# A four-layer attention and feed-forward kernel: a woven instruction order for the second and third layer, and narrow probability-times-value products in the fourth attention

## The reference

```
x = x + attn0(LN(x), ctx)   # 16 heads of 96, 4 key heads, keys = ctx and x
x = x + ffn0(LN(x))         # ternary weights, inner size 1376, cut to int8
x = x + attn1(LN(x), ctx)   # softmax(x ctx^T) ctx, no weights
x = x + ffn1(LN(x))         # z = x A^T; top 16 of 64 experts gate z; B z
x = x + attn2(LN(x), ctx)   # Q = x Wq^T + bq, K = ctx Wk^T + bk, values = ctx
x = x + ffn2(LN(x))         # three experts, two of them used, with gates
x = x + attn3(LN(x), ctx)   # RMS norm, 32 heads of 16 over 8 key heads, 64 keys
x = x + ffn3(LN(x))         # NF4 quantised and dequantised weights, inner 1376
```

## Time and profile before

| what | value |
|---|---|
| median of the runs | 1604.14 us |
| the profiled execution itself | 1597.06 us |
| its span, first to last instruction | 1595.2 us |
| mean granted TensorE clock | 0.935 of full |
| PE busy | 1379.0 us, 86% |
| DVE busy | 1016.7 us, 64% |
| ACT busy / POOL busy | 461.2 us / 294.1 us |
| 16 DMA engines | 60 GB/s over the span |

### The profile page before, as it was taken

One profiled execution on the slowest core, in us unless ns is written; L12 is line 12 of the kernel. 1 busy time (PEld: TensorE's weight loads), 2 busy tenths in 40 slices (PEclk: granted clock), 3 DMA queues, 4 the chain that ended last, 5 costly groups with the idle time before them and its releaser, 6 DMA issues.

```text
span 1595.2 us, 18304 instructions
## 1 busy us (share of the span) xinstructions
PE 1379.0 (86%) x6285; PEld 1062.4 (67%) x6285; DVE 1016.7 (64%) x2281; ACT 461.2 (29%) x993; POOL 294.1 (18%) x170
## 2 busy tenths in 40 slices
PE   6559999999899998989966778689997777898998
PEld 5437776777677767867755457567886455677876
DVE  4567777767877775654587766773467499744241
ACT  3224334333333532422333102223213332321010
POOL 4101111111111211211112002215423311022120
PEclk9779999999999999999985899789998899899999
DMA  5521223313222331232112102200111100011001
GB/s 187 180 82 47 79 57 105 81 56 95 75 56 66 89 94 50 58 79 71 45 34 69 58 22 60 71 19 27 53 53 54 39 0 1 1 53 53 24 19 53
DMA packets 99405, 96.37 MB, mean 60 GB/s; under 512 B 13138, under 2 KB 72418, under 8 KB 99314
## 3 DMA queue, kind: packets, MB, share of 16 engines
q1 hardware_dynamic: 98802, 94.35, 20.2%
q0 software_dynamic: 512, 0.85, 0.2%
HBM read 84.34 MB, written 10.82 MB: 60 GB/s over the span
## 4 chain that ended last, share of the span: by engine, by line
PE 63%; DVE 23%; issue 5%; DMA 3%; ACT 3%; SPq 3%; POOL 1%; ACTq 0%; DVEq 0%
PE bank L1688 47%; PE bank L2050 5%; PE bank L1782 4%; DVE nf_y L1630 4%; SPq L772 2%; DVE xn L1193 2%; PE bank L1715 1%; PE bank L1772 1%; DVE mx L1545 1%; PE bank L2013 1%; POOL slots L818 1%; DVE st L1266 1%; DVE st L1175 1%; DMA nf_a<-in_L_w 1%; DVE e L1548 1%
## 5 line engine op out<-in xcount | busy, mean ns | idle before, releaser
L1688 PE MATMUL bank<-xT,slots 128*128 128x512 f32 (+1 forms) x1920 | 459.7, 397 | 4.0 <-DVE xT L1152 2.1
L818 POOL TENSOR_TENSOR slots<-staging,slots 128x1024 fp32r<-128x1024 f32 (+4 forms) x97 | 228.4, 2357 | 1035.9 <-ACT slots L911 1035.9
L1688 PEld LDWEIGHTS bank<-xT,slots 128*128 128x128 f32 (+1 forms) x1920 | 349.5, 183 | 100.0 <-issue 7.6
L1630 DVE TENSOR_SCALAR nf_y<-nf_w 128x512 fp32r<-128x512 f32 (+2 forms) x495 | 252.3, 537 | 29.2 <-PE bank L2050 28.1
L1688 PE MATMUL bank<-slots,h 128*128 128x512 f32 (+1 forms) x728 | 179.9, 407 | 15.9 <-DVE h L1292 9.7
L2050 PE MATMUL bank<-nf_y,nf_d 128*128 128x512 f32 (+2 forms) x495 | 164.3, 415 | 13.7 <-DVE nf_y L1630 10.7
L1688 PEld LDWEIGHTS bank<-slots,h 128*128 128x128 f32 (+1 forms) x728 | 141.5, 195 | 52.0 <-DVE h L1292 10.5
L911 ACT ACTIVATE slots<-staging 128x1024 fp32r<-128x1024 f32 (+4 forms) x97 | 98.2, 1019 | 189.0 <-PE bank L1688 174.7
L945 ACT ACTIVATE e<-bank,mx 128x320 f32<-128x320 f32 x128 | 66.4, 523 | 235.4 <-DVE mx L1230 235.0
L2050 PEld LDWEIGHTS bank<-nf_y,nf_d 128*128 128x128 f32 (+1 forms) x495 | 92.6, 191 | 51.5 <-issue 19.1
L1782 PE MATMUL bank<-eT,v 128*96 128x256 f32 (+1 forms) x384 | 110.0, 408 | 0.3
(11 more groups left out here) (247 smaller groups left out, 1716.9 us busy)
## 6 DMA issues: line engine op xcount, KB each, us to landing
staging<-in_L_wqkT SPq DMA_DIRECT2D x16, 480.0 KB, 3.8
nf_out<-nf_w SPq DMA_DIRECT2D x30, 256.0 KB, 2.1
staging<-nf_out SPq DMA_DIRECT2D x30, 256.0 KB, 2.9
staging<-in_L_woT SPq DMA_DIRECT2D x16, 384.0 KB, 3.7
staging<-in_L_w SPq DMA_DIRECT2D x12, 512.0 KB, 3.9
nf_a<-nf_max SPq DMA_DIRECT2D x40, 128.0 KB, 3.5
nf_r<-nf_rcp SPq DMA_DIRECT2D x40, 128.0 KB, 3.4
nf_w<-in_L_w SPq DMA_DIRECT2D x15, 256.0 KB, 4.2
```

The lines of the kernel that those rows point to most:

```text
L818: g.tensor_tensor(lo, split_source(i), hi.bitcast(FP32), ALU.subtract).then_inc(*sig.mark("weight_low", i))
L1630: v.tensor_scalar(nf_y[0:rows, i % STAIR_RING, 0:size], w_, bound, first, compare, ALU.mult)\
L1688: ins = mm(dst, l_, r_, start=i == 0, stop=i == len(passes) - 1)
```

## The change

1. `schedule()` is rewritten for layers 1 and 2. `k2`, `c2`, `m2`, `c2t`, `z1(0)`, `route1(0)` and `gates1(0)` now stand inside attention 1. `turn(4,0)`, `raw1(2,0)`, `raw1(2,1)` and their `scores1` stand inside the last tiles of `z1/zt1/b1`. The chunks of `k2` and `m2` are loaded ahead of the others. In attention 2 both `stats` chains come early, and the first four `hid2` are those of half 0.
2. Waits and buffers: `h2` is four tiles instead of one; the wait of gate2 and of ACT's first `hid2` for the last NF4 store is now a wait of DVE at `hid2(0,0,1)`; `b1c` is loaded early; some tiles change their place.
3. Attention 3: seven of the eight `q3` products are spread, six of them over the first five units and one ahead of them. `scale3` is gone. `turn3` transposes the unscaled exponentials. `pv3` now makes, for each token tile and head pair, one product with `eT3` as stationary side and 34 columns of `vd3` moving: 32 value columns and 2 columns of ones, which give the sums. DVE takes the reciprocal of those sums and scales the result (`af3`), and the new step `back3` transposes it with 2 transposes a unit; ACT and DVE split that as `pv3` did.

```diff
 
-    steps += [("raw1", 1, 0), ("raw1", 1, 1), ("scores1", 1, 0), ("scores1", 1, 1), ("turn", 2, 1), ("probs1", 1, 0),
-              ("raw1", 1, 2), ("pv1", 1, 0), ("probs1", 1, 1), ("scores1", 1, 2), ("pv1", 1, 1), ("stats", 3, 0),
-              ("raw1", 1, 3), ("probs1", 1, 2), ("scores1", 1, 3), ("pv1", 1, 2), ("turn", 3, 0), ("probs1", 1, 3),
-              ("raw_route1", 0), ("pv1", 1, 3), ("stats", 3, 1)]
+    steps += [("k2", 0), ("raw1", 1, 0), ("raw1", 1, 1), ("k2", 1), ("scores1", 1, 0), ("bias2",), ("k2", 2),
+              ("scores1", 1, 1), ("turn", 2, 1), ("probs1", 1, 0), ("k2", 3), ("raw1", 1, 2), ("pv1", 1, 0),
+              ("probs1", 1, 1), ("raw1", 1, 3), ("c2",), ("scores1", 1, 2), ("pv1", 1, 1), ("stats", 3, 0),
+              ("m2", 0), ("probs1", 1, 2), ("scores1", 1, 3), ("m2", 1), ("pv1", 1, 2), ("m2", 2), ("turn", 3, 0),
+              ("raw_route1", 0), ("probs1", 1, 3), ("z1", 0), ("c2t",), ("route1", 0), ("pv1", 1, 3), ("m2", 3),
+              ("gates1", 0), ("stats", 3, 1)]
     if only == 3:
         return steps
 
-    steps += [("route1", 0), ("turn", 3, 1), ("raw_route1", 1), ("z1", 0), ("gates1", 0)]
+    after = {0: [("turn", 3, 1), ("raw_route1", 1)], 1: [("route1", 1)], 2: [("gates1", 1)],
+             4: [("stats", 4, 0)], 6: [("turn", 4, 0), ("raw1", 2, 0), ("raw1", 2, 1)],
+             7: [("scores1", 2, 0), ("scores1", 2, 1)]}
     for t in range(TILES):
-        if t + 1 < TILES:
-            steps.append(("z1", t + 1))
-        steps.append(("zt1", t))
-        if t >= 1:
-            steps.append(("b1", t - 1))
-        if t < 2:
-            steps.append(("route1", 1) if t == 0 else ("gates1", 1))
-        if t - 1 == TPH - 1:
-            steps.append(("stats", 4, 0))
-    steps += [("b1", TILES - 1)] + [("k2", c) for c in range(KT)] + [("bias2",), ("c2",), ("turn", 4, 0), ("stats", 4, 1)]
+        steps += [("z1", t + 1)] * (t not in (0, 6, 7)) + [("zt1", t)] + [("b1", t - 1)] * (t > 0) + after.get(t, [])
+        steps += [("z1", t + 1)] * (t in (0, 6))
+    steps += [("probs1", 2, 0), ("b1", TILES - 1), ("stats", 4, 1)]
     if only == 4:
         return steps
 
-    steps += [("m2", c) for c in range(KT)] + [("c2t",)]
-    steps += [("raw1", 2, 0), ("raw1", 2, 1), ("scores1", 2, 0), ("scores1", 2, 1), ("turn", 4, 1), ("probs1", 2, 0),
-              ("raw1", 2, 2), ("pv1", 2, 0), ("probs1", 2, 1), ("scores1", 2, 2), ("pv1", 2, 1), ("stats", 5, 0),
-              ("raw1", 2, 3), ("probs1", 2, 2), ("scores1", 2, 3), ("pv1", 2, 2), ("turn", 5, 0), ("probs1", 2, 3),
-              ("raw_gate2", 0), ("pv1", 2, 3), ("stats", 5, 1)]
+    steps += [("pv1", 2, 0), ("probs1", 2, 1), ("pv1", 2, 1), ("stats", 5, 0), ("turn", 4, 1), ("raw1", 2, 2), ("raw1", 2, 3),
+              ("scores1", 2, 2), ("scores1", 2, 3), ("turn", 5, 0), ("raw_gate2", 0), ("probs1", 2, 2), ("gate2", 0),
+              ("pv1", 2, 2), ("probs1", 2, 3), ("hid2", 0, 0, 0), ("pv1", 2, 3), ("stats", 5, 1)]
...
-    steps += [("gate2", 0), ("hid2", 0, 0, 0), ("turn", 5, 1), ("hid2", 0, 0, 1), ("raw_gate2", 1), ("gate2", 1)]
-    for i in range(2 * (KT - 1)):
-        steps += [("moe", i)] * (i < 4) + [("hid2", 0, 1 + i // 2, i % 2)]
+    steps += [("hid2", 0, c, 0) for c in range(1, KT)] + [("turn", 5, 1), ("raw_gate2", 1), ("hid2", 0, 0, 1), ("gate2", 1)]
+    steps += [("moe", 0), ("hid2", 0, 1, 1), ("moe", 1), ("hid2", 0, 2, 1), ("moe", 2), ("hid2", 0, 3, 1), ("moe", 3)]
...
-    steps += [("q3", 0, 0), ("turn", 6, 1)] + [("q3", c, 0) for c in range(1, KT)] + [("q3", c, 1) for c in range(KT)]
+    steps += [("q3", 0, 0), ("turn", 6, 1), ("q3", 1, 0)]
+    queries = {0: [("q3", 2, 0), ("q3", 3, 0)], **{c + 1: [("q3", c, 1)] for c in range(KT)}}
     units = [(b, c) for b in range(B) for c in range(KT)]
     steps.append(("keys3", 0, *units[0]))
     for n in range(len(units) + TURN3_LAG + 1):
         if n < len(units):
             steps.append(("scores3", n, *units[n]))
-        if 1 <= n <= len(units):
-            steps.append(("scale3", n - 1))
+            steps += queries.get(n, [])
+        if n > TURN3_LAG + 1:
+            steps.append(("back3", n - TURN3_LAG - 2, *units[n - TURN3_LAG - 2]))
         if n > TURN3_LAG:
             steps.append(("pv3", n - TURN3_LAG - 1, *units[n - TURN3_LAG - 1]))
         if 1 <= n <= len(units):
             steps.append(("values3", n - 1, *units[n - 1]))
         if TURN3_LAG <= n < len(units) + TURN3_LAG:
             steps.append(("turn3", n - TURN3_LAG, *units[n - TURN3_LAG]))
+        if n > TURN3_LAG + 1:
+            steps.append(("low3", n - TURN3_LAG - 2, *units[n - TURN3_LAG - 2]))
         if n > TURN3_LAG:
             b, c = units[n - TURN3_LAG - 1]
-            if b >= 1 and c < TPB:
-                steps.append(("o3", TPB * (b - 1) + c))
-            if (b, c) == (BPH, TPB - 1):
+            if b >= 1 and 1 <= c <= TPB:
+                steps.append(("o3", TPB * (b - 1) + c - 1))
+            if (b, c) == (BPH, TPB):
                 steps.append(("stats", 7, 0))
             if (b, c) == (BPH, KT - 1):
                 steps.append(("turn", 7, 0))
         if n + 1 < len(units):
             steps.append(("keys3", n + 1, *units[n + 1]))
+    steps += [(step, len(units) - 1, *units[-1]) for step in ("back3", "low3")]
...
+            chunk(("k2", i), P, (2, D), [((slice(None),), by_k(a["L2_wkT"], 2 * i, 2 * i + 2))])
...
-        for name, ap in (("z1", a["L1_aT"]), ("b1", a["L1_bT"]), ("k2", a["L2_wkT"]), ("m2", a["L2_wq"])):
+        for name, ap in (("m2", a["L2_wq"]), ("z1", a["L1_aT"]), ("b1", a["L1_bT"])):
...
-        h2 = sb("h2", [P, 2, 2, KT, TOK], F32R, l)
-        hf2 = sb("hf2", [P, 2, HALF], FP32, l)
+        h2 = {}
+        for block in ((0, 1), (1, 0), (1, 1)):
+            h2[block] = sb("h2_{}_{}".format(*block), [P, 2, KT, HALF], F32R, l)
...
+        sb("between", [P, 2330], FP32, l)
+        h2[0, 0] = sb("h2_0_0", [P, 2, KT, HALF], F32R, l)
+        hf2 = sb("hf2", [P, 2, HALF], FP32, l)
...
-        vd3 = sb("vd3", [P, 2, PAIRS, P], FP32, l)
+        vd3 = sb("vd3", [P, 2, PAIRS, PAIR3], FP32, l)
...
+        rc3 = sb("rc3", [P, TPB * PAIRS, 2], FP32, l)
+        af3 = sb("af3", [P, 2, TPB, P], FP32, l)
...
+                                     ("b1c", b1c[:], a["L2_b1"]),
...
+                    pool.wait_ge(*sig.when("vd3_clear", 0))
+                    for j in range(2):
+                        g.memset(vd3[CTX * j:CTX * (j + 1), :, :, 2 * HD3 + j], 1.0).then_inc(*sig.mark("vd3_ones", j))
+                        pool.wait_ge(*sig.when("vd3_ones", j))
...
-                i = (e * KT + c) * 2 + hf
-                if i == 0:
-                    for q in range(2):
-                        act.wait_ge(*sig.when(f"nf4_stored{q}", 3 * FT - 2 + (3 * FT - q) % 2))
+                i = 2 * KT * e + (hf * KT + c if e == 0 else 2 * c + hf)
                 act.wait_ge(*sig.when("hid2_product", (e, c, hf)))
                 act.wait_ge(*sig.when("loaded_b1c", 0))
                 if i >= 2:
                     e_, r_ = divmod(i - 2, 2 * KT)
-                    act.wait_ge(*sig.when("h2_low", (e_, r_ // 2, r_ % 2)))
+                    act.wait_ge(*sig.when("h2_low", (e_, r_ % KT, r_ // KT) if e_ == 0 else (e_, r_ // 2, r_ % 2)))
...
+                if (e, c, hf) == (0, 0, 1):
+                    for q in range(2):
+                        dve.wait_ge(*sig.when(f"nf4_stored{q}", 3 * FT - 2 + (3 * FT - q) % 2))
...
-            def scale3(n):
-                for i in range(TPB):
-                    dve.wait_ge(*sig.when("exp3", (n, i)))
-                    e = e3[:, n % E3_RING, i].rearrange("p (h k) -> p h k", h=HPC)
-                    hs = slice(i * HPC, (i + 1) * HPC)
-                    link(v.tensor_reduce(sm[:, n % 4, hs], e, AX.X, ALU.add))
-                    link(v.reciprocal(mx[:, n % 4, hs], sm[:, n % 4, hs]))
-                    v.tensor_tensor(e, e, mx[:, n % 4, hs].unsqueeze(2).broadcast_to((P, HPC, CTX)), ALU.mult)\
-                        .then_inc(*sig.mark("probs3", (n, i)))
-
             def pv3(n, b, c):
-                low("pv3", n, a3[:, b % 2, 1, c], psum(("pv3", n))[:, 0:S], a3[:, b % 2, 0, c])
+
+                dve.wait_ge(*sig.when("pv3_product", n))
+                pairs = psum(("pv3", n))[:, 0:TPB * PAIRS * PAIR3].rearrange("p (q m) -> p q m", m=PAIR3)
+                link(v.reciprocal(rc3[:], pairs[:, :, 2 * HD3:]))
+                if n >= 2:
+                    dve.wait_ge(*sig.when("back3_product", n - 2))
+                v.tensor_tensor(af3[:, n % 2].rearrange("p i (q h d) -> p (i q) h d", q=PAIRS, h=2),
+                                pairs[:, :, 0:2 * HD3].rearrange("p q (h d) -> p q h d", h=2),
+                                rc3[:].unsqueeze(3).broadcast_to((P, TPB * PAIRS, 2, HD3)), ALU.mult)\
+                    .then_inc(*sig.mark("scaled3", n))
+
+            def low3(n, b, c):
```

(19 more changed lines are left out.)

53 lines of the change are left out of this document (25 added, 28 removed), and 2 rows, old and new, of the table LAYER_STAGES.

## The result

| | before | changed |
|---|---|---|
| time, median of five runs each | 1605.4 us (1601.9 to 1609.4) | 1592.7 us (1588.8 to 1594.7) |
| ratio of the runs | 1 | 0.9923, 95% interval 0.9901 to 0.9946 |
| profiled execution, span | 1595.2 us | 1587.0 us |
| busy PE / DVE / ACT / POOL | 1379 / 1017 / 461 / 294 us | 1377 / 973 / 461 / 294 us |
| mean granted clock | 0.935 | 0.933 |

What follows compares the result with a forecast made beforehand. It took layers 1 and 2 to be bound by chains hopping between PE, ACT and DVE, and attention 3 by DVE, then PE. 1597.1 minus 24.5 minus 24 is 1548.6, scaled to 1555 us; range 1532 to 1582.

Steps and rivals of the forecast that it cites:

- unit of attention 3: Attention 3's loop: PE needs 4.5 us a unit, DVE about 4.2; the old unit was about 6.6 us.
- attention 3, stretch: From 1232.2 to the last `o3`: 116.6 us of PE plus 19 of waits, 136 us against 160.5 before.
- attention 3, whole: Attention 3 gains 24.5 us; bounds 9 to 32.
- k2, m2, c2 out of the open stretch: Behind the last `b1`: their 13 us of PE move into attention 1's idle time; PE pays nothing, DVE 3 us.
- `raw1(2,..)` into the loop, attention 2 rewoven: The turn, two `raw1` and scores cost the `zt1`/`b1` loop 5 us of PE; attention 2 becomes about 1 us worse.
- the NF4 jobs shift by a few: Background NF4 jobs move slightly along the schedule; counted as nothing.
- woven order in sum: Layers 1 and 2: 33 - 5 - 3 - 1 = 24 us gained; bounds 0 and 35.
- the narrow product gains PE nothing: Attention 3: stationary loads make the narrow product's passes take 1.8 us a unit, against 1.73 for the old values product.
- The first stall on the keys: Start of attention 3: `keys3(0)` stands behind a POOL split, so PE waits 5.3 us, plus 1.5 for half clock.
- attention 3's list of waits: Attention 3: first keys 5.3 and 1.5 us, `stats(7,0)` 4.5 and 1.7, end of loop 6; 19 us in all.
- 33 us leave the place: Behind the last `b1`: 28 us of k2, c2, turn, m2 and a DVE wait, plus 5.0 of `raw1`, leave the open stretch.
- My bound of 0: Layers 1 and 2 gain nothing, every filled gap returning as a DVE wait; rival "Only attention 3 pays", 15%, 1580 us.

Runs made afterwards that it cites:

- e5: e1 with each unit's masked keys handed out earlier, ahead of the weight splits on POOL: ratio to before 0.9860, 10.1 us better than e1.
- e1: The kernel before with the edits of attention 3 alone: ratio to before 0.9923, 12.3 us faster.
- e12: e9 with the old order again behind the last `b1` and in attention 2, k2, m2, c2 still in attention 1: ratio to before 0.9756, 1561.2 us.
- e9: The changed kernel with both repairs, NF4 jobs as in e3 and keys as in e5: ratio to before 0.9810, 18.1 us better than the changed kernel.
- e4: The kernel before with its sum of room fixed at 609.4, the changed kernel's value, which shifts its NF4 jobs: ratio to before 1.0088, 14.1 us slower.
- e3: The changed kernel with the sum of room fixed at 611.4, the old value: ratio to before 0.9885, 6.1 us better than the changed kernel.
- e2: The changed kernel with attention 3 as before: ratio to before 1.0021, 3.4 us slower.
- e18: e12 with each product of k2 and m2 made twice on PE, and through a shared helper those of `k3`: ratio to before 0.9763, 1.1 us over e12.
- e13: The kernel before with each product of k2 and m2 made twice at the old place, `k3`'s too: ratio to before 1.0024, 3.8 us slower.
- e11: e9 with one round instead of three in the statistics' reciprocal square root, `stats(2,0)` to `stats(5,1)`: ratio to before 0.9727, 13.3 us faster than e9.
- e7: e3 with the passage from attention 1 to the gated product ordered as before, k2, m2, c2 staying in attention 1: ratio to before 0.9891, no different from e3.

## Why the prediction was wrong, step by step

| step of the forecast | forecast | measured |
|---|---|---|
| unit of attention 3 | 4.5 us | 4.55 us |
| attention 3, stretch | 136 us | 146.8; 135.3 with keys ahead (e5) |
| attention 3, whole | -24.5 | -12.3 (e1); -22.4 (e5) |
| k2, m2, c2 out of the open stretch | part of -24 | -16.7 (e12 against e5, with the new order of `hid2` in it) |
| `raw1(2,..)` into the loop, attention 2 rewoven | -5 of PE to pay, about 1 worse | +8.7 (e9 against e12) |
| "the NF4 jobs shift by a few" | 0 | +14.1 (e4), 6.1 back in e3 |
| woven order in sum | -24 | +3.4 (e2); -8.0 with the NF4 jobs at their old places (e9 against e5) |

**Right.** DVE's sums leave, the bound of attention 3 passes to PE, and the narrow product gains PE nothing: 1.71 us against my 1.8. The issue-gap rule of the Trainium skill (TensorE: Matmul & The Clock Gate, Back-to-back issue gap) would have had 0.4 us there, and the measured 0.107 us per pass with its own stationary load decides for the rows. The first stall on the keys was 5.10 us, forecast 5.3. The end of the loop was 1.9 us of wait and 1.4 of clock, where I had 6. And PE indeed paid nothing in attention 1 for k2 and m2 (92.5 us with them doubled, e18, 92.9 without, e12).

**The first step that failed** is in one half-sentence: that the NF4 jobs' shift counts nothing. It was put at nothing without a reason, and cost 14.1 us by e4 and 6.1 by e3. The jobs are strung along the steps by a running sum of room. The new order ended that sum 2.0 lower, and jobs moved by a place or so all along the list, hundreds of us ahead of the edit. One of them has a DMA wait of 9 us on DVE (already in the trace of before), harmless only for what PE has queued between. I had counted the jobs moved and not looked at what each of them waits for.

**The second** is attention 3's list of waits. I looked for keys behind splits at the start only. The filler holds the query weights' slots until 1278, so the splits that need these slots come in mid-loop, ahead of the keys of the next unit. Two more waits, 6.0 us together. And I charged the restart at half clock for two waits (1.5 and 1.7 us), where it came behind five groups of waits, at 1.4 to 2.9 us each. Work of 116.6 us with 19 of waits and clock was the forecast; measured are 30 beside it.

**The third** is the bound of layers 1 and 2, and the largest miss: 24 us were forecast, 8.0 measured with the NF4 jobs at their old places. "33 us leave the place" was a sum of PE's time. e18, e13 and e11 say that PE's time there is worth little and DVE's about all of it. `stats(4,1)` used to lie beside `raw1(2,0)` and `raw1(2,1)`, 7 us of PE; woven, these went to a loop that had no room, and the statistics stood bare: 11.0 us, about three of them, by estimate, because a split on POOL ran beside (last section). My bound of 0 ("every filled gap returns as a DVE wait") was nearer the truth for this half than the 24; I gave it 15%. That all of the 13 us ahead of `zg` was the order of `route1(0)` and `gates1(0)`, as I read it from the trace of the changed kernel, fell too (e7): it is DVE's sum, not the order.

**The sum** from the measured parts: -12.3 (attention 3), -16.7, +8.7, +14.1 (or +6.1 by e3) gives -6 to -14; measured are -12.5. It is a rough check, since these parts come from kernels that differ in more than one thing.

What stays open is why e4 loses 8 us more than e3 gains. The single traces put 4.5 of them ahead of `turn(2,0)`, of which the moved splits of k2 may be 3, and 3.6 behind it; no run separates them. Open is also what the doubling of k2 and m2 alone costs, since no run doubles them without `k3`.

## What to carry to other kernels

Before counting what a reordering moves, list what it moves without meaning to: background jobs, splits and loads placed by a running sum or by "as late as possible". For each that shifts, ask what it waits for and what its engine's neighbours then have queued; a wait that is harmless in one place (9.3 us on DVE, 1.5 on PE) was 9.0 us on PE a place or two earlier, and the shift cost 14 us in all. Where two engines hop, find out which one's microseconds count, by doubling one's work and cutting the other's, before filling the holes of either, and look in the trace where else a doubled helper is used. And put small work that the next step needs ahead of big work that something later needs on the same in-order queue: two lines of order gave 10 us, the rewritten attention 12.

## What the runs showed of the hardware that I had not expected

- 34-column float32 products with a 128-column stationary load each go at 0.107 us per pass (16 records in 1.71 us), and PE's granted clock stays at its upper level among them: 1.00 from 1299.9 to 1345.0.
- The granted clock behind a short wait went both ways. A wait of only 2.3 us is followed by scores at 3.4 us instead of 1.72, half speed, and the two waits of 0.8 and 1.1 us around the last `back3` by 7.1 us for what takes 5.7. But the same two waits in e12 are followed by 5.7 us, and 3.3 us ahead of `q3(0,0)` in the changed kernel (1223.43) by 12 records in 2.99 us at a granted clock of 1.00. So a short wait can cost most of its length again, and doesn't always.
- A split on POOL slows small DVE work more than I had seen in the earlier trace rows. DVE of the changed kernel ahead of the 11 us wait, with splits from 1015.97 to 1018.3 and from 1019.14 to 1021.5:

```profile
1016.03 3.26 DVE L1639 TENSOR_SCALAR nf_y<-nf_w 96x512 fp32r<-96x512 f32 x3
1019.21 0.68 DVE L1183 BATCH_NORM_STATS2 st<-x 128x6 f32<-128x512 f32 x1
...
1020.34 1.18 DVE L1188 TENSOR_SCALAR rt<-mv 128x4 f32<-128x4 f32 x1
```

  Three steps take 3.26 us, where two took 0.74 just before, and a 4-column instruction 1.18 instead of 0.17; `BATCH_NORM_STATS2` beside the second split keeps its time.
- Twenty small DMA issues from one queue take 12.6 us (0.6 to 0.7 each), longer than one of them needs to land (3.1 us by the median). DVE goes on 1.5 us behind the last issue, so it waits mostly for the last one's turn in the queue, and less for its landing.
